# A Mamba and mixture-of-experts layer: the order of the expert tiles, and the last stage moved between them

## The reference

```
x = x + A(layernorm(x))                 # A(v) = v + mamba(layernorm(v) * g + b)
x = x + F(layernorm(x))

F(v): logits = v @ Wg + bg              # 8 experts
      two largest logits of a token, softmax over the two
      h  = relu(v @ W1[e] + b1[e])      # 512 wide
      eo = h @ W2[e] + b2[e]            # 256 wide
      y  = v + sum of the two chosen experts' eo, weighted
      gamma * (y - mean) / sqrt(var + eps) + beta
```

## Time and profile before

| | |
|---|---|
| median of 3 runs (lowest, highest) | 2411.43 us (2410.77, 2414.64) |
| the profiled execution | 2398.82 us |
| its span, first to last instruction | 2397.1 us |
| mean granted TensorE clock | 0.962 |
| PE, share of the span | 90% |
| DVE | 87% |
| POOL | 76% |
| ACT | 67% |

### The profile page before, as it was taken

How to read it: one execution, slowest core, us unless ns; L and a number is a source line. 1 busy time by engine, 2 the same in 40 slices (tenths; PEclk the granted TensorE clock), 3 DMA queues, 4 the chain that set the end, 5 groups by cost and what they waited for, 6 DMA issues and landing times. The chain is left out here.

```text
span 2397.1 us, 48455 instructions
## 1 busy us (share of the span) xinstructions
PE 2166.0 (90%) x13451; PEld 1751.9 (73%) x13452; DVE 2095.3 (87%) x3172; ACT 1611.5 (67%) x3293; POOL 1826.9 (76%) x1093
## 2 busy tenths in 40 slices
PE   8889899999989898999999898989877999999980
PEld 5667677677777777777677777777666899999970
DVE  5999999999998999999999989998994677777768
ACT  6687877878787868778787878687752333333326
POOL 3888989889898989898898989898983444444447
PEclk9999999999999999999999999999988999999995
DMA  5031413324140413233241404131326566666558
GB/s 175 8 135 50 137 64 115 107 71 147 40 160 19 160 50 132 67 116 105 73 138 49 158 21 160 48 131 47 132 80 206 86 92 92 95 94 92 91 84 279
DMA packets 228968, 245.95 MB, mean 103 GB/s; under 512 B 111843, under 2 KB 193795, under 8 KB 228676
## 3 DMA queue, kind: packets, MB, share of 16 engines
q1 hardware_dynamic: 183108, 191.97, 26.2%
q0 software_dynamic: 25584, 34.62, 8.3%
q10 hardware_dynamic: 20112, 17.32, 2.2%
HBM read 180.50 MB, written 63.32 MB: 102 GB/s over the span
## 5 line engine op out<-in xcount | busy, mean ns | idle before, releaser
L858 POOL TENSOR_TENSOR dbu<-drive_u,w_all 128x1024 f32<-128x1024 f32 x384 | 904.3, 2364 | 88.4 <-DVE ps_a L663 35.8
L1162 ACT ACTIVATE ps_a<-delta,a_neg 128x512 f32<-128x512 f32 x768 | 517.3, 685 | 136.0 <-DVE ss L663 119.3
L875 POOL TENSOR_TENSOR wp<-ss,rows_c 128x1024 f32<-128x1024 f32 x192 | 453.8, 2364 | 38.4 <-DVE ss L663 37.8
L1775 POOL DMA_INDIRECT acc_scratch<-ow,idx x135 | 210.1, 1556 | 283.9 <-DMA acc_scratch<-ow,idx 148.7
L675 DVE TENSOR_TENSOR wd<-ps_a,rows_c 128x1024 f32<-128x1024 f32 x320 | 382.6, 1196 | 0.0
L1440 PEld LDWEIGHTS ps_y<-ident,wd 128*128 128x128 f32 x2560 | 302.8, 144 | 99.8 <-issue 70.0
L1440 PE MATMUL ps_y<-ident,wd 128*128 128x128 f32 x2560 | 341.6, 279 | 13.3 <-DVE wd L675 13.3
L1467 PEld LDWEIGHTS ps_a<-dg,duT 128*128 128x128 f32 x2048 | 254.1, 200 | 57.6 <-issue 55.4
L1467 PE MATMUL ps_a<-dg,duT 128*128 128x128 f32 x2048 | 263.5, 284 | 30.2 <-ACT carry L1169 27.4
L1893 PEld LDWEIGHTS e_ps_h<-xT,ee 128*128 128x128 f32 x2160 | 260.6, 192 | 14.8 <-DVE xT L1689 8.3
L1893 PE MATMUL e_ps_h<-xT,ee 128*128 128x128 f32 x2160 | 264.7, 276 | 2.9 <-DVE xT L1689 2.8
(11 more groups left out here) (200 smaller groups left out, 3595.0 us busy)
## 6 DMA issues: line engine op xcount, KB each, us to landing
rows_c<-b_scratch SPq DMA_DIRECT2D x128, 512.0 KB, 4.9
w_all<-b_scratch SPq DMA_DIRECT2D x96, 512.0 KB, 4.0
xt<-xs_scratch SPq DMA_DIRECT2D x540, 32.0 KB
xb<-in_L_attn_x_dram SPq DMA_DIRECT2D x16, 512.0 KB, 4.1
hx<-in_L_attn_x_dram SPq DMA_DIRECT2D x16, 512.0 KB, 6.4
x_scratch<-hx SPq DMA_DIRECT2D x16, 512.0 KB, 2.9
acc_scratch<-stage SPq DMA_DIRECT2D x16, 512.0 KB, 2.9
r_x<-x_scratch ACTq DMA_DIRECT2D x32, 256.0 KB
```

Source lines behind the costliest of these rows:

```text
L858: pool.tensor_tensor(dbu[:, k % NBU], du[:, g % 2, :].unsqueeze(1).broadcast_to([P, 2, CH]), bb[:, row:row + 2, :], ALU.mult).then_inc(dbu ...
L875: pool.tensor_tensor(wp[:, s % 2], ss[:, s % 2], cc[:, rows, :], ALU.mult).then_inc(wp_done, 1)
L1162: act.activation(dst, dl[:, g, :], ACT.Exp, scale=a_neg[:, g, n:n + 1]).then_inc(exp_done, 1)
L1775: pool.indirect_dma_start(out=acc_dram, out_offset=bass.IndirectOffsetOnAxis(ap=idx[:, old, :], axis=0), in_=ow[:, old, :], in_offset=None ...
```

## The change

1. **Order of the tiles.** `CUTS = (11, 14)`. The table is made in two parts. After chunk 10 the full tiles of that time are known; the first 81 (`early_tiles`) make the early table, in small operations spread over the steps of the first block (`EARLY_AT`, `early_step`), with two short matmuls. The other 54 tiles stand in three passes over the experts: tiles begun before chunk 11, before chunk 14, and the rest. So tokens of chunks 0 to 10 are complete after 95 tiles at most, those of chunks 11 to 13 after 119. Behind the last chunk the chain of table operations works on 24 segments instead of tiles.
2. **The last stage between the tiles.** 28 of the 32 pieces (chunks 0 to 13) are handled in steps 101 to 134 (`PIECE_AT`). In each such step SyncE loads piece c, VectorE gathers c and scales c-3, ScalarE normalises c-2, makes the factors for a pair of pieces and stores c-5, GpSimd makes offsets and finishes c-4. Four pieces follow after the last tile. Steps from 81 on are written out, since the loop now ends there (18 turns).
3. **Half the maxima on ScalarE.** Two of the four blocks of the first layer go to ScalarE (`Relu` with the bias); PSUM is laid out so that the two engines read different banks.
4. Normalised rows stay in `ee` in SBUF (8 buffers instead of 16), the weights' double buffer and the table have memory of their own, and the residual's slices are loaded in 18 loop turns and 14 steps.

ScalarE, before: two steps of the written-out part (`turned_h` holds the table, TENSOR_LOAD reads a register from it, L1815 is the weight copy).

The diff, cut to its core:

```diff
+CUTS = (11, 14)
...
+def early_tiles(nt, experts):
+    return CUTS[0] * 2 * nt - experts + 1
...
+        EARLY_AT = [CUTS[0] * SG + at for at in (47, 48, 50, 51)] + [(CUTS[0] + 1) * SG + at for at in range(46, 54)] + [
+            c * SG + 47 for c in CUTS[1:]]
...
+                if at in EARLY_AT:
+                    early_step(EARLY_AT.index(at))
...
-            dve.wait_ge(counts_made, 3)
             dve.wait_ge(*routed(NC - 1, 13))
-            link(dve.tensor_tensor(over, cnt[:].unsqueeze(2).broadcast_to([P, E, T]),
-                                   jf.unsqueeze(1).broadcast_to([P, E, T]), ALU.is_gt))
...
+            link(count_tiles(NK, base))
...
+            link(dve.tensor_scalar(passed_by, ends[:, 1:], idf[:, 0, 0:1], None, ALU.is_le))
+            link(dve.tensor_tensor(jump, passed_by, jump, ALU.mult))
+            link(dve.tensor_reduce(jumped[:], jump, AX.X, ALU.add))
...
-    PEEL = LAG + 5 + (NTT - LAG - 5) % RING
-    TURNS = (NTT - PEEL) // RING
+    PEEL = LAG + 5 + (NE - LAG - 5) % RING
+    TURNS = (NE - PEEL) // RING
...
-    SLOTS = 6
-    LOADS = 16
+    SLOTS = 4
+    LOADS = 8
+    LAST_PIECE = CUTS[-1] * NT // CT
+    BATCHES = [*((c, 2) for c in range(0, LAST_PIECE, 2)), *((c, 1) for c in range(LAST_PIECE, PIECES))]
+    BEFORE = [CUTS[k] * 2 * NT + E - 1 for k in range(len(CUTS))] + [NTT]
+    PIECE_AT = [101 + c * 35 // LAST_PIECE for c in range(LAST_PIECE)]
...
-            for s in range(NTT, NTT + LAG):
+            eng.wait_ge(tab_r, 15)
+            for s in range(NE, NTT + LAG):
                 body(s, s % RING)
+                if TURNS + s - NE < PIECES:
+                    extra(TURNS + s - NE)
+            for c in range(LAST_PIECE, PIECES + 6):
+                rest(c)
...
+            def load_piece(c):
+                if there(c):
+                    k = next(k for k in range(len(CUTS) + 1) if k == len(CUTS) or c < CUTS[k] * NT // CT)
+                    if c == (CUTS[k - 1] * NT // CT if k else 0):
+                        for slot in range(RING):
+                            sync.wait_ge(t_out[slot], 16 * len(range(slot, BEFORE[k], RING)))
+                    b = c % LOADS
+                    if c >= LOADS:
+                        sync.wait_ge(scaled, c - LOADS + 1)
+                    sync.dma_start(ee[:, b].rearrange("p (i d) -> p i d", i=CT), rows_of(acc_t, c)).then_inc(c_in[b], 16)
...
-                    for j in range(KF):
-                        ins = dve.tensor_scalar(hT[:, 1 - par, j, :], ps_h[:, 1 - par, j, :],
+                    for j in range(KF // 2):
+                        ins = dve.tensor_scalar(hT[:, 1 - par, j, :], inner(1 - par, j),
                                                 b1t[:, bass.ds(e * KF + j, 1)], 0.0, ALU.add, ALU.max)
...
+                if real(s - 1):
+                    t = s - 1
+                    e = act.value_load(tabi[0:1, 1, bass.ds(t, 1)], min_val=0, max_val=E - 1)
+                    wait(act, h_full, 1, t, 1)
+                    wait(act, o_full, 1, t, -1)
+                    for j in range(KF // 2, KF):
+                        ins = act.activation(hT[:, 1 - par, j, :], inner(1 - par, j), ACT.Relu,
+                                             bias=b1t[:, bass.ds(e * KF + j, 1)])
+                    ins.then_inc(h_act, 1)
+                for c in pieces_at(s):
+                    piece_step(c)
```

335 lines of the change are left out of this document (209 added, 126 removed).

## The result

The changed kernel took **2419.91 us** in the median of 15 runs (2415.23 to 2423.62), the kernel before 2411.68 in 15 runs beside it (2406.56 to 2417.78): a ratio of 1.0033, 95% interval 1.0025 to 1.004. It is slower by 8.2 us where 20.9 us less were forecast. On another occasion, where the kernel before takes 2397.7 us, the changed one took 2416.35: 1.0076 (1.0061 to 1.0092).

The account below looks back on a forecast made before the run. It took VectorE as busiest in the first stage and TensorE as full in the tile stage, with 61.5 us after the last landing. +2, +20.5 and -43.4 sum to -20.9, from 2411.43 to 2390.5 us; range 2366 to 2409.

Parts of the forecast that it names:

- The tail, -43.4: Behind the last landing: four remaining pieces take 18.1 us in place of 61.5, so -43.4 us.
- The tables, +2: First stage: 15 small VectorE operations for early tables at 0.19 us each, partly hidden, cost +2 us.
- The junction, 0: Between first block and tiles: the new table chain on VectorE ends under cover of GpSimd's last scatters, 0 us.
- Tile order and straight code, 0 and up to +5: Tile stage: more expert changes delay scatters but output slots absorb it, 0 us; up to +5 if they overrun.
- The steps with pieces, +20.5: Steps 101 to 134: ScalarE becomes the bound at 4.16 us a step, VectorE and GpSimd hidden, +20.5 us.
- +37, if every second normalise also waits 2 us or more for its offsets: Steps 101 to 134, upper end: ScalarE's normalise waits for offsets GpSimd computes behind a scatter, +37 us.
- VectorE's sum, 3.55: Steps 101 to 134: VectorE's work with two maxima gone and pieces added, 3.55 us a step, hidden.
- Everybody waits for everybody: Mutual-waits rival, steps with pieces: ScalarE awaits offsets, GpSimd landings; 4.65 us a step, +37, total 2407; chance 0.09.
- TensorE bound: Rival: TensorE stays the bound in the tile stage, ScalarE needing only 3.0 us a tile; total 2370; chance 0.26.
- Crowded DMA: Rival, steps with pieces: scatters land in 6.6 us, +64, total 2434; sign: landings well over 4 us; chance 0.11.
- The clock: Rival, steps with pieces: TensorE's waits drop its clock to 1.2 GHz, +120 us, total some 2490; chance 0.04.
- What bounds the kernel: Tile stage of the kernel before: TensorE is full, 3.56 us a tile, all but never waiting.

Follow-up runs that it names:

- r2: The changed kernel, unchanged, profiled on the same chip as the kernel before; 2416.35 us, ratio to before 1.0076.
- e5: The kernel before plus 14 VectorE instructions of 128x8 in the first block, each adding two SBUF tensors; ratio 1.0049.
- e6: The kernel before plus 14 VectorE instructions at the same first-block steps, each reading one SBUF tensor; ratio 1.0004.
- e14: The kernel of e4 with early tables made in one go in the routing step, one operand of two-input instructions in PSUM; 2383.7 us, ratio 0.9883.
- r1: The kernel before, unchanged, profiled on the same chip as r2 and r3; 2397.5 us, ratio 0.9998.
- e1: The changed kernel with all four maxima of a tile on VectorE again; ratio to before 1.0039.
- e15: The kernel of e14 with all four maxima of a tile on ScalarE; 2378.5 us, ratio to before 0.9864.
- r3: The kernel of e4, unchanged, on the same chip as r1 and r2; 2382.6 us, ratio to before 0.994.
- e4: The changed kernel with the pieces' offsets and residual adds moved from GpSimd to VectorE; 2391.5 us, ratio to before 0.9908.
- e10: The changed kernel with only the residual adds moved from GpSimd to VectorE; ratio to before 0.9982.
- e11: The changed kernel with only the offsets moved from GpSimd to VectorE; ratio to before 1.0016.
- e8: The kernel before with one more turn of four tiles in straight code ahead of the loop; ratio 0.9989.
- e2: The changed kernel with the tile index made by a VectorE instruction reading one tensor instead of two; 2416.7 us, ratio 1.0019.

## Why the prediction was wrong

The direction was wrong, and the time lies 29 us above the forecast and 11 above the range. By its own steps:

- **The tail, -43.4: right.** On one chip it was -41.3. From the last scatter's issue (2390.36 in r2) its landing takes 3.7 us, and 19.4 follow it where 18.1 were worked out, in the forecast's order: statistics, factors, normalise, scaling, four queued additions. In the earlier trace rows 61.5 followed. The change does what it says.
- **The tables, +2: mis-sized, 10.1 measured.** "Each like its other small ones at 0.19 us" was the step that failed. The one in that row has an operand in PSUM. A VectorE instruction with two inputs in SBUF, or a scaling from SBUF to SBUF, can be held until GpSimd's tensor instruction is over, and the next one too, up to 4.07 us there, and VectorE is the first block's bound, so the holds are on the path (e5, e6, e14). The junction, 0, was right: from the last gate to tile 0 it is 38.2 us in r1 and 34.9 in r2, 35.9 and 36.6 in the first two profiles.
- **Tile order and straight code, 0 and up to +5: 7.3 measured.** Scatters held up nobody, as forecast. Missed was that the residual loads, one in four tiles in a loop, come one a tile in straight code, and that load and add follow each other there: 4.0 us a tile for 14 tiles, +5.4, of which tiles 95 to 101 give 1.5 back. The other 3.4 lie in tiles 0 to 81, whose cause is open. The 4.53 us priced for a change of expert was misread: by the earlier trace rows that gap ended on VectorE's result, not on a landing.
- **The steps with pieces, +20.5: the step that decided, 42.5 measured** (35.9 in the first profile). Its terms for ScalarE were fair one by one (a maximum 0.36, pair 0.62, normalise 0.59), but it never was the bound: e1 took two maxima off it and the window grew by 3.0 us, e15, beside a GpSimd that only scatters, put two more on it and the window shrank by 2.4. The end named for this term, "+37, if every second normalise also waits 2 us or more for its offsets", is what happened: 13 waits, 45.7 us. "GpSimd: 1.86 for a scatter, some 0.4 for a table read, 0.82 x (1.27 + 0.1): 3.4, hidden" failed, in "hidden" and not in its prices: GpSimd is busy 90.1 of 156 us in r2, 58%. But its sum has no wait for landings. 21 scatters wait 2.2 us each for one (47.0 us), and offset and add stand in that queue. VectorE's sum, 3.55, left out the holds: 32 index instructions take 28.7 us in place of 4.8. The argument against the mutual waits, "with ScalarE late the offsets are early", assumed the bound it was to test. Moving offsets and adds off GpSimd takes 31.5 of the 42.5 us away (r3); the other 11.0 are open.
- **Rivals.** "Everybody waits for everybody", given 0.09, is the mechanism of the larger part (e4, e10, e11); it forecast 4.65 us a step and 4.62 (first profile) and 4.84 (r2) were measured. That it comes so near is partly luck, since it had neither the holds nor the 11.0 us that r3 keeps. It came out at 2407 only because the first block was priced at +2. With the 10.1 and 7.3 measured it gives 2422. TensorE bound: no. Crowded DMA: at most a part. The pieces' loads landed in 3.0 us (median) and the engines were 67% busy, but the scatters that GpSimd waited for in the window landed 4.4 us behind their issue (r2, median of 26) where r1 has 3.8, a sign that the forecast had named; that is far from the 6.6 of this rival. By an estimate from these rows it is 26 x 0.6, 16 us at most, and no run takes it alone. The clock: 0.98 in the first profile and 0.92 in r2, where TensorE waited up to 6.6 us at a stretch; its second-layer matmuls were 394 ns there and 379 in r1. That can be a part of the 7 us by which r2's window is the longer; the first profile has most of the loss at a clock of 0.98.
- **What bounds the kernel, "TensorE is full": half right.** It holds for the kernel before (e8). SyncE issues a tile in nearly the same time, 3.53 us, and in the changed kernel's first profile, at 3.68 us a tile, the chain of waits between 1945 and 1965 us runs over SyncE alone.

The Trainium skill, "SBUF — State Buffer", section "Who interferes with whom", has the rule that this forecast should have weighed: VectorE and GpSimd share a pair of SBUF ports under an exclusive lock, taken by a VectorE instruction with two SBUF inputs against a GpSimd instruction that reads SBUF, and by copies and tensor_scalar in their two-port mode. The runs agree: two inputs held to the end of GpSimd's add (1044 ns for 150), a reduction with one input never (142 ns), a tensor_scalar from SBUF to SBUF held for 1.97 us (128x8) and for 1.03 in the mean (128x256, e2), one of 128x1 not (204 ns). A hold can outlast the instruction that began it: 4.07 us beside two multiplies in a row. The rule of the Trainium skill, "ScalarE: Activation LUTs", section "Rules for kernel authors", that the forecast cited against maxima on ScalarE isn't borne out here: a pair of maxima takes 0.61 us on VectorE and 0.62 on ScalarE, and e15, with all four there, is as fast as e14 within the noise (0.9864 against 0.9883).

## What to carry to other kernels

When work moves beside other work, price each instruction by a row in which the engines it will then run beside are doing what they will be doing, VectorE and GpSimd above all; a 1-element instruction can cost 2 us. Where an edit takes a hold off one instruction, look whether the next one has it (e2). An engine that waits for its own DMAs in queue order (here GpSimd, for the landing of scatters) should not carry what another engine waits for: taking two short jobs off it turned +0.8% into -0.6%, and the early tables in another form and place gained some 0.25% more. And profile both kernels side by side on the same chip before reading a difference in pace as an effect of the change.

## What was unexpected in the hardware

- The hold lasts to the end of GpSimd's tensor instruction, over two of them if they follow each other (4.07 us), and shows up as the *duration* of VectorE's, not as idle time: 14 probes of 128x8 cost 15.4 us with two inputs and 2.0 with one.
- A GpSimd instruction behind a scatter begins in the record some 0.55 us before the scatter ends: its add shows 1.85 us and its 128x4 offset 0.78, with VectorE idle too (2392.74 and 2392.89), but an offset ends 0.23 us behind the scatter and an add 1.30, or 1.22 behind an offset. GpSimd can be held in turn: behind the last tile its 128x2 offset took 0.19 us three times and 0.72 the fourth (2406.08), when it ended 0.05 us behind VectorE's scaling with two inputs (2406.75).
- Two occasions differ by 0.6% on the kernel before (2397.7 and 2412.6 us). In the changed kernel the difference shows in SyncE's gap between two tiles' DMAs, 1.16 us in r2 and 1.30 in the first profile (means of some 60 between 1900 and 2120 us), with the same instructions. Why, and whether it is the chip, these runs don't tell.
